# Softmax denominators: a VectorE reciprocal in place of two ScalarE activations

## The chip, the cores and the metric

One Trainium2 chip, all 8 of its cores, one launch. The metric is the device time of the slowest core in microseconds. Each core works on 1024 of the 8192 tokens: four cores share one batch element, and the program of all eight is the same.

## The reference

A "macaron" layer: `x += 0.5*ffn(ln(x))`, `x += attn(ln(x))`, `x += 0.5*ffn(ln(x))` on x of shape 2 x 4096 x 2048, f32. Only the attention matters here:

```
latent_k = h @ Wk.T ; latent_v = h @ Wv.T          # 64 latent dimensions
q_latent = einsum('bthd,hdl->bthl', Q, q_to_latent)  # 16 heads
logits   = q_latent . latent_k / sqrt(64), causal,
           plus 0.5 * (sum of q_latent) * (sum of latent_k) / sqrt(64) in a band of 64 keys
attn     = softmax(logits)
ctx      = attn @ (latent_v @ v_up) ; out = ctx @ Wo.T
```

The softmax's division is the place of the change: the kernel sums the exponentials of each query and multiplies the context row by one over the sum.

## The kernel before

The activations are held transposed, features on partitions and the core's 1024 tokens along the free dimension. A first phase does, for each of the four token blocks of its batch element, layernorm, ffn, layernorm and the latent k and v. Then come the query projection, the attention, the output projection and the second ffn.

The attention runs over 16 heads, and in each head over 32 key tiles `i` of 128 keys plus two iterations to drain. The order of work on each engine is the order in which the helpers are called, since every engine takes its instructions in order and engines meet only at semaphores (`ct` counts TensorE's steps, `cs` ScalarE's, `cv` VectorE's). In iteration `i`:

- VectorE: `emit_outer` (L1363, `ob`) and `emit_select` (L1377, `mr`) make the band term. They need nothing of this iteration.
- TensorE, `emit_iter`: the context product of tile i-2 into `CV` (L1450, keys on the contraction, 65 output rows: 64 of the context and, as row 64, the sum of the exponentials), then the scores of tile i into `PC` (L1471).
- ScalarE copies the 256 leading columns of the scores to SBUF (L1391), VectorE adds the band term (L1399, `madd`), ScalarE takes the exponential of these (L1426) and, without the detour, of the rest (L1419).

A query tile's work ends early, by causality: the columns 0 to 511 of `CV` are complete after tile 19, the columns 512 to 1023 after tile 31. So each head has two epilogues, one for each half of the columns:

- `emit_epi_sums`: VectorE copies 64 rows of `CV` to `cv_sb` (L1277) and the sums to `sums_sb` (L1279, 1x512). Then ScalarE makes the reciprocal as exp(-ln(s)), with two activations on one partition, L1286 (`Ln`) and L1289 (`Exp`), into `rcp_row`.
- `emit_epi_rep`: TensorE multiplies a column of ones with `rcp_row`, so that all 128 partitions hold it (L1304, f32, 1x512, two passes that the trace shows as x2), and VectorE copies that to `rep_sb` (L1311).
- `emit_epi_out`: TensorE multiplies `cv_sb` with `v_up` (L1326), and VectorE multiplies the product with `rep_sb` into `bbuf` (L1337).

For half 0 the three are called at i = 22, 24 and 25 of the same head, ahead of that iteration's own work. For half 1 all three are called together at i = 1 of the next head, ahead of iteration 1 (in the last head, behind everything). There TensorE's order is: the scores of tile 0 of the new head, L1304 and L1326 of the epilogue, then the scores of tile 1. The first step on the head after that, L1083 (called at i = 2), waits for L1337 too. Stages of the next head's queries and bounds (`emit_A_stage`) are spread over i = 2 to 15.

A single table set with `Ln` and `Exp` is loaded once at the start (`preload_set6`, L632).

Of the kernel before, what the change touches and what calls it, by code (L numbers as in the profile page):

```python
# [12 lines left out]
AF = mybir.ActivationFunctionType  # L13
# [624 lines left out]
def build_fused():  # L638
# [38 lines left out]
    with contextlib.ExitStack() as stx:  # L677
# [10 lines left out]
        block = e(nc.Block())  # L688
        preload_set6(block)
        ct, cs, cv = S['ct'], S['cs'], S['cv']  # L690
# [7 lines left out]
        with contextlib.ExitStack() as ph1:  # L698
# [50 lines left out]
            for j in range(4):  # L749
                xq_toks = []  # L750
                for qd in range(4):
# [5 lines left out]
                    def _(sy, j=j, qd=qd, rel=rel, dxn=dx.n):  # L757
                        sy.wait_ge(dx.h, dxn)
                        if rel is not None:
# [7 lines left out]
                _, ln1_ap, mr1 = emit_ln(nc, block, bufs, S, x_chunks, xhat,  # L767
                                         wait0=w0, mrr=mrr1)
# [6 lines left out]
                _, ln2_q, mr2 = emit_ln(nc, block, bufs, S, x_chunks, xhat,  # L775
                                        wait0=w2l, mrr=mrr2)
# [64 lines left out]
        with contextlib.ExitStack() as attn_stack:  # L841
# [21 lines left out]
            sums_sb = ea(nc.sbuf_tensor("sums_sb", [1, NTOK], F32))  # L863
            rep_sb = ea(nc.sbuf_tensor("rep_sb", [128, NTOK], F32))
            rcp_row = ea(nc.sbuf_tensor("rcp_row", [1, NTOK], F32))
# [151 lines left out]
            with contextlib.ExitStack() as ps2:  # L1017
# [252 lines left out]
                def emit_epi_sums(h, half, sc_tok):  # L1270
                    lo, hi = 512 * half, 512 * half + 512
                    @block.vector
                    def _(v, sc_tok=sc_tok, lo=lo, hi=hi,
                          cl=PF['ctx_last']):
                        v.wait_ge(ct.h, sc_tok)
                        v.wait_ge(ct.h, cl)
                        v.tensor_copy(cv_sb[:, lo:hi],  # L1277
                                      CV[0:64, lo:hi]).then_inc(cv.h, 1)
                        v.tensor_copy(sums_sb[:, lo:hi],  # L1279
                                      CV[64:65, lo:hi]).then_inc(cv.h, 1)  # L1280
                    cv.inc(1)
                    s_tok = cv.inc()
                    @block.scalar
                    def _(s, s_tok=s_tok, lo=lo, hi=hi):
                        s.wait_ge(cv.h, s_tok)
                        s.activation(rcp_row[:, lo:hi], sums_sb[:, lo:hi],  # L1286
                                     AF.Ln).then_inc(cs.h, 1)
                        s.wait_ge(cs.h, cs.n + 1)
                        s.activation(rcp_row[:, lo:hi], rcp_row[:, lo:hi],  # L1289
                                     AF.Exp, scale=-1.0).then_inc(cs.h, 1)  # L1290
                    cs.inc(1)
                    return (s_tok, cs.inc())

                def emit_epi_rep(h, half, rcp_tok):
                    lo, hi = 512 * half, 512 * half + 512
                    nxt = A.get(h + 1)
                    ve_war = nxt['b8'] if nxt else 0
                    @block.tensor
                    def _(t, rcp_tok=rcp_tok, ve_war=ve_war, lo=lo, hi=hi,
                          pdf=PF['pdfree']):  # L1300
                        t.wait_ge(cs.h, rcp_tok)
                        t.wait_ge(cv.h, ve_war)
                        t.wait_ge(cv.h, pdf)
                        t.matmul(PA[:, lo:hi], bufs['onesr_f'][:, :],  # L1304
                                 rcp_row[:, lo:hi], start=True,
                                 stop=True).then_inc(ct.h, 1)
                    rep_tok = ct.inc()
                    @block.vector
                    def _(v, rep_tok=rep_tok, lo=lo, hi=hi):
                        v.wait_ge(ct.h, rep_tok)  # L1310
                        v.tensor_copy(rep_sb[:, lo:hi],  # L1311
                                      PA[:, lo:hi]).then_inc(cv.h, 1)
                    return (rep_tok, cv.inc())
# [32 lines left out]
                for h in range(H):  # L1346
# [132 lines left out]
                    for i in range(NT + 2):  # L1479
                        if i == 1 and epi.get('pend') is not None:  # L1480
                            ph, psc = epi.pop('pend')
                            s1 = emit_epi_sums(ph, 1, psc)
                            r1 = emit_epi_rep(ph, 1, s1[1])
                            co1 = emit_epi_out(ph, 1, r1, s1[0],
                                               PF['pdfree'])
                            PF['pdfree'] = co1
                            PF['pb'] = (cv.h, s1[0])
                            PF['pa'] = (cv.h, co1)
                        if h + 1 < H and 2 <= i <= 15:
                            emit_A_stage(h + 1, i - 2)  # L1490
                        if i == 22:
                            epi['sums0'] = emit_epi_sums(h, 0, sc_toks[19])
                        elif i == 24:
                            epi['rep0'] = emit_epi_rep(h, 0,
                                                       epi['sums0'][1])
                        elif i == 25:
                            out0 = emit_epi_out(h, 0, epi['rep0'],
                                                epi['sums0'][0],
                                                PF['pdfree'])
                            PF['pdfree'] = out0  # L1500
# [13 lines left out]
                    if h + 1 < H:  # L1514
                        epi['pend'] = (h, sc_toks[NT - 1])
                    else:
                        s1 = emit_epi_sums(h, 1, sc_toks[NT - 1])
                        r1 = emit_epi_rep(h, 1, s1[1])
                        ctxout_tok = emit_epi_out(h, 1, r1, s1[0],
                                                  PF['pdfree'])  # L1520
# [29 lines left out]
        with contextlib.ExitStack() as f2:  # L1550
# [13 lines left out]
            def wo_cb(m, pap, mm_tok):  # L1564
# [14 lines left out]
            _, ln3_ap, mr3 = emit_ln(  # L1579
                nc, block, bufs, S, x_chunks, xhat3,  # L1580
                wait0=[(cv.h, wo_toks[c]) for c in range(NCH)], mrr=mrr3)
# [98 lines left out]
```

## Time and profile before

| | |
|---|---|
| runs | 3282.74, 3283.88 (median), 3368.11 us |
| profiled execution | 3286.02 us, span of its slowest core 3283.4 us |
| spans of the 8 cores | 3267.2 to 3283.4 us, granted clock 0.747 to 0.749 |
| VectorE busy over the span | 1254.8 us (38%), 2561 instructions |
| ScalarE busy over the span | 869.3 us (26%), 1789 instructions |
| TensorE busy over the span | 2431.0 us (74%), 8607 matmuls |

The share of busy time is an average over stages. The page also prints the span in 40 slices of 82.1 us with one digit each, the busy tenths of an engine in that slice; the attention fills the slices from about the 21st to the 35th. A timeline row gives the start, the duration, the engine, the line, the operation with output and input, and in brackets how long the engine had been idle before it, with what released it.

### The profile page before, as it was taken

To read this page: it belongs to the slowest core of one execution; us is meant where nothing else is said; L and a number is where in the kernel's file an instruction comes from. 1 tells how busy PE (TensorE), PEld (TensorE's weight loads), DVE (VectorE), ACT (ScalarE), POOL (GpSimd) and SP (SyncE) were. 2 spreads that over 40 slices of the span, in tenths; PEclk is the share of its full clock that TensorE was granted. 3 is DMA by queue.
4 is the path that set the end of the run, shared out by engine and by line. 5 is a ranking of instruction groups with operands and counts; after the bars stand their busy time and mean duration, and the time that the engine had idled before them with its cause. 6 is when DMAs were issued, how large, how long until landed. Compare 5 with 4: busy or idle time off the path is not lost.

```text
span 3283.4 us, 29191 instructions; the slowest of 8 cores (3267.2 to 3283.4 us)
## 1 busy us (share of the span) xinstructions
PE 2431.0 (74%) x8607; PEld 863.0 (26%) x8607; DVE 1254.8 (38%) x2561; ACT 869.3 (26%) x1789; POOL 52.2 (2%) x78
## 2 busy tenths in 40 slices
PE   5998669866988679849736666666666666597997
PEld 1333124321432133313212111112221111142333
DVE  2103320243003320331157676666776676412103
ACT  2110211022102201010015455545555554402110
POOL 0000000000000000000000000000000000000000
PEclk8999889887999789979855555555555555598999
DMA  4440334114330344014100000000000000221332
GB/s 128 66 71 1 106 52 77 26 32 120 57 52 0 106 77 77 0 26 69 27 17 1 1 1 1 1 1 1 1 1 1 1 1 1 48 55 19 68 68 102
DMA packets 15263, 127.97 MB, mean 39 GB/s; under 512 B 6433, under 2 KB 6746, under 8 KB 7626
## 3 DMA queue, kind: packets, MB, share of 16 engines
q0 software_dynamic: 6864, 82.28, 14.8%
q1 hardware_dynamic: 8250, 43.83, 3.7%
q8 instruction: 77, 1.26, 0.2%
q14 instruction: 72, 0.59, 0.1%
HBM read 196.53 MB, written 9.27 MB: 63 GB/s over the span
## 4 chain that ended last, share of the span: by engine, by line
PE 58%; DVE 22%; issue 7%; ACT 7%; DMA 4%; DVEq 1%; ACTq 0%; POOL 0%; SPq 0%; POOLq 0%
PE bp_p L319 24%; DVE xhat L243 5%; PE fe_p L574 5%; PE fe_p L516 4%; PE ln_sum L184 4%; PE ln_sum L187 4%; DVE madd L1399 3%; ACT madd L1391 3%; DVE mr L1377 2%; PE CV L1450 2%; PE PA L1304 2%; PE PC L1471 2%; PE bp_p L332 2%; PE bp_cs L289 1%; DVE madd L1200 1%
## 5 line engine op out<-in xcount | busy, mean ns | idle before, releaser
L319 PE MATMUL bp_p<-xhat,wslotP 128*128 128x512 bf16 x2560 | 574.6, 383 | 56.3 <-DVE xhat L243 56.3
L1450 PE MATMUL CV<-probs,vtT 128*65 128x512 bf16 (+3 forms) x768 | 343.7, 512 | 253.2 <-ACT probs L1426 252.6
L1471 PE MATMUL PC<-qlat_h,kaug 65*128 65x512 bf16 (+3 forms) x768 | 348.3, 522 | 8.4 <-DMA qlat_h<-crow_bf 8.4
L319 PEld LDWEIGHTS bp_p<-xhat,wslotP 128*128 128x128 bf16 x2560 | 245.9, 99 | 383.1 <-issue 104.6
L177 ACT ACTIVATE ln_sq<-x_res 128x1024 bf16<-128x1024 f32 x144 | 152.2, 1057 | 723.4 <-DVE x_res L584 317.5
L1426 ACT ACTIVATE probs<-madd 128x256 bf16<-128x256 f32 (+1 forms) x512 | 206.5, 403 | 352.6 <-DVE madd L1399 343.6
L1399 DVE TENSOR_TENSOR madd<-madd,mr 128x256 f32<-128x256 f32 (+1 forms) x512 | 209.3, 409 | 174.5 <-ACT madd L1391 120.6
L359 ACT ACTIVATE bbuf<-bp_p,b_sb 128x1024 bf16<-128x1024 f32 x80 | 89.2, 1114 | 673.5 <-PE bp_p L332 673.5
L1450 PEld LDWEIGHTS CV<-probs,vtT 128*65 128x65 bf16 x768 | 96.4, 134 | 528.8 <-issue 526.0
L1391 ACT ACTIVATE madd<-PC 128x256 f32<-128x256 f32 (+1 forms) x512 | 183.7, 359 | 180.5 <-PE PC L1471 178.9
L1377 DVE COPY_PREDICATED mr<-bandm_sb,ob 128x256 bf16<-128x256 uint8 (+1 forms) x512 | 210.4, 411 | 54.6 <-DVE ob L1363 2.3
L1419 ACT ACTIVATE probs<-PC 128x640 bf16<-128x640 f32 (+5 forms) x384 | 205.8, 536 | 0.0
L413 DVE TENSOR_SCALAR ffn_zsb<-kv_ps,b_sb 8x1024 f32<-8x1024 f32 x4 | 5.1, 1272 | 440.0 <-PE kv_ps L403 440.0
L243 DVE TENSOR_TENSOR xhat<-x_res,ln_rrep 128x1024 bf16<-128x1024 f32 x144 | 163.7, 1211 | 24.1 <-PE ln_rrep L233 24.1
L184 PE MATMUL ln_sum<-x_res,ones_f 128*1 128x512 f32 x288 | 147.9, 595 | 17.7 <-DMA x_res<-xall 9.8
L187 PE MATMUL ln_sum<-x_res,ones_f 128*1 128x512 f32 x288 | 147.9, 595 | 0.0
L1363 DVE TENSOR_SCALAR ob<-qshrepb,ksumT 128x256 bf16<-128x256 bf16 (+1 forms) x512 | 140.8, 275 | 0.0
L1304 PE MATMUL PA<-rcp_row,onesr_f 1*128 1x512 f32 x64 | 65.3, 1121 | 93.1 <-ACT rcp_row L1289 66.9
L200 DVE TENSOR_SCALAR ln_m<-ln_sum 1x1024 f32<-1x1024 f32 x9 | 10.9, 1211 | 320.0 <-PE ln_sq L193 320.0
L319 PE MATMUL bp_p<-bbuf,wslotF 128*128 128x512 bf16 x512 | 113.2, 385 | 18.2 <-DMA wslotF<-woq 18.2
L574 PE MATMUL fe_p<-ffn_vx,wslotP 128*128 128x512 bf16 x512 | 120.1, 400 | 6.6 <-DVE ffn_vx L556 6.6
L1471 PEld LDWEIGHTS PC<-qlat_h,kaug 65*128 65x128 bf16 x768 | 96.0, 128 | 100.4 <-issue 91.9
(170 smaller groups left out, 2010.6 us busy)
## 6 DMA issues: line engine op xcount, KB each, us to landing
x_res<-xall SPq DMA_DIRECT2D x16, 2048.0 KB, 9.0
wslotP<-w1q POOLq DMA_DIRECT2D x16, 2048.0 KB, 16.6
wslotP<-varr POOLq DMA_DIRECT2D x4, 2048.0 KB, 16.1
wslotP<-uarr POOLq DMA_DIRECT2D x4, 2048.0 KB, 16.0
wslotP<-wqq POOLq DMA_DIRECT2D x4, 2048.0 KB, 16.6
wslotF<-woq POOLq DMA_DIRECT2D x4, 2048.0 KB, 14.6
wslotF<-w1q POOLq DMA_DIRECT2D x4, 2048.0 KB, 13.9
yout<-x_res SPq DMA_DIRECT2D x4, 2048.0 KB
```

The source lines that it names most:

```text
L184: t.matmul(p_sum[:, 0:512], bufs['ones_f'][:, 0:1], src_chunks[c][:, 0:512], start=(c == 0), stop=(c == NCH - 1))
L187: t.matmul(p_sum[:, 512:1024], bufs['ones_f'][:, 0:1], src_chunks[c][:, 512:1024], start=(c == 0), stop=(c == NCH - 1))
L243: v.tensor_mul(dst[:, NTOK * c:NTOK * (c + 1)], src_chunks[c], p_rrep[:, :]).then_inc(cv.h, 1)
L319: mi = t.matmul(P[par][:, 512 * half:512 * half + 512], lhsT, rhs_sb[:, NTOK * k + 512 * half: NTOK * k + 512 * half + 512], start=(k == 0 ...
L574: mi = t.matmul(P[par][:, 512 * half:512 * half + 512], lhsT, vx[:, NTOK * j + 512 * half: NTOK * j + 512 * half + 512], start=(j == 0), s ...
L1377: v.copy_predicated(mr_sb[r][:, 0:lead], bandm_sb[:, 256 * r:256 * r + lead], ob_sb[i % 2][:, 0:lead]).then_inc(cv.h, 1)
L1391: s.activation(madd2_sb[i % 2][:, 0:lead], PC[:, qlo + dlt:qlo + dlt + lead], AF.Copy).then_inc(cs.h, 1)
L1399: v.tensor_tensor(madd2_sb[i % 2][:, 0:lead], madd2_sb[i % 2][:, 0:lead], mr_sb[i % 4][:, 0:lead], ALU.add).then_inc(cv.h, 1)
L1419: s.activation(probs[i % 2][:, a:b], PC[:, a + dlt:b + dlt], AF.Exp).then_inc(cs.h, 1)
L1426: s.activation(probs[i % 2][:, qlo:qlo + lead], madd2_sb[i % 2][:, 0:lead], AF.Exp).then_inc(cs.h, 1)
L1450: mi = t.matmul(CV[0:65, a:b], vtT[:, 66 * j:66 * j + 65], probs[j % 2][:, a:b], start=(j == 0), stop=last)
L1471: mi = t.matmul(PC[:, a + dlt:b + dlt], kaug[0:65, 128 * i:128 * i + 128], ql[0:65, a:b], start=True, stop=True)
```

## The change

In `emit_epi_sums` the two ScalarE activations are taken out. In their place VectorE does one `reciprocal` on the same 1x512 row, from `sums_sb` into `rcp_row`, directly behind its copy of the sums and with a wait for that copy. The function returns a token of VectorE's semaphore, and `emit_epi_rep` makes TensorE wait for that one.

```diff
                         v.tensor_copy(sums_sb[:, lo:hi],
                                       CV[64:65, lo:hi]).then_inc(cv.h, 1)
+                        v.wait_ge(cv.h, cv.n + 2)
+                        v.reciprocal(rcp_row[:, lo:hi],
+                                     sums_sb[:, lo:hi]).then_inc(cv.h, 1)
                     cv.inc(1)
                     s_tok = cv.inc()
-                    @block.scalar
-                    def _(s, s_tok=s_tok, lo=lo, hi=hi):
-                        s.wait_ge(cv.h, s_tok)
-                        s.activation(rcp_row[:, lo:hi], sums_sb[:, lo:hi],
-                                     AF.Ln).then_inc(cs.h, 1)
-                        s.wait_ge(cs.h, cs.n + 1)
-                        s.activation(rcp_row[:, lo:hi], rcp_row[:, lo:hi],
-                                     AF.Exp, scale=-1.0).then_inc(cs.h, 1)
-                    cs.inc(1)
-                    return (s_tok, cs.inc())
+                    return (s_tok, cv.inc())
...
-                        t.wait_ge(cs.h, rcp_tok)
+                        t.wait_ge(cv.h, rcp_tok)
                         t.wait_ge(cv.h, ve_war)
                         t.wait_ge(cv.h, pdf)
```

## Rows read from the trace of the kernel before

**Rows 1.** The page's part 2: busy tenths and granted clock, 40 slices

```profile
DVE  2103320243003320331157676666776676412103
ACT  2110211022102201010015455545555554402110
PEclk8999889887999789979855555555555555598999
```

**Rows 2.** Busy time by stretch: attention's main part; length, busy by engine, clock

```profile
1740.00:2850.00 1110.00, 719.88 (x1807) 222.10 (x1807) 762.80 (x1943) 571.48 (x1453) 15.08 (x16) 0.50 0.00 1
```

**Rows 3.** Groups by line and shape, 1480 to 2850 us: busy, mean ns | idle before

```profile
L1304 PE MATMUL PA<-rcp_row,onesr_f 1*128 1x512 f32 x64 | 65.3, 1121 | 93.1 <-ACT rcp_row L1289 66.9 <-ACT madd L1391 26.2
L1289 ACT ACTIVATE rcp_row<-rcp_row 1x512 f32<-1x512 f32 x32 | 20.1, 629 | 2.9
L1286 ACT ACTIVATE rcp_row<-sums_sb 1x512 f32<-1x512 f32 x32 | 20.1, 629 | 30.2 <-DVE sums_sb L1279 30.2
```

**Rows 4.** Timeline at a head's start: epilogue of half 1

```profile
2132.89 0.68 DVE L1279 COPY sums_sb<-CV 1x512 f32<-1x512 f32 x1
2133.66 0.63 ACT L1286 ACTIVATE rcp_row<-sums_sb 1x512 f32<-1x512 f32 x1 [0.89 <-DVE sums_sb L1279]
2134.38 0.63 ACT L1289 ACTIVATE rcp_row<-rcp_row 1x512 f32<-1x512 f32 x1
...
2135.37 2.04 PE L1304 MATMUL PA<-rcp_row,onesr_f 1*128 1x512 f32 x2 [4.19 <-ACT rcp_row L1289]
...
2137.52 0.69 DVE L1311 COPY rep_sb<-PA 128x512 f32<-128x512 f32 x1 [3.95 <-PE PA L1304]
...
2139.01 0.38 ACT L1391 ACTIVATE madd<-PC 128x256 f32<-128x256 f32 x1 [4.00 <-PE PC L1471]
```

**Rows 5.** Timeline of the same head's iterations 22 and 23: half 0

```profile
2113.69 0.69 DVE L1279 COPY sums_sb<-CV 1x512 f32<-1x512 f32 x1
...
2114.30 0.27 DVE L1363 TENSOR_SCALAR ob<-qshrepb,ksumT 128x256 bf16<-128x256 bf16 x1
2114.47 0.63 ACT L1286 ACTIVATE rcp_row<-sums_sb 1x512 f32<-1x512 f32 x1 [0.89 <-DVE sums_sb L1279]
2114.67 0.43 DVE L1377 COPY_PREDICATED mr<-bandm_sb,ob 128x256 bf16<-128x256 uint8 x1
2115.19 0.63 ACT L1289 ACTIVATE rcp_row<-rcp_row 1x512 f32<-1x512 f32 x1
2115.73 0.36 ACT L1391 ACTIVATE madd<-PC 128x256 f32<-128x256 f32 x1
...
2116.18 2.04 PE L1304 MATMUL PA<-rcp_row,onesr_f 1*128 1x512 f32 x2 [1.63 <-ACT madd L1391]
2116.25 0.43 DVE L1399 TENSOR_TENSOR madd<-madd,mr 128x256 f32<-128x256 f32 x1 [1.15 <-ACT probs L1419]
...
2117.63 0.42 DVE L1399 TENSOR_TENSOR madd<-madd,mr 128x256 f32<-128x256 f32 x1 [0.23 <-ACT probs L1419]
...
2118.32 0.69 DVE L1311 COPY rep_sb<-PA 128x512 f32<-128x512 f32 x1 [0.27 <-PE PA L1304]
```

**Rows 6.** Groups by line and shape, VectorE, whole span: same columns as rows 3

```profile
L1399 DVE TENSOR_TENSOR madd<-madd,mr 128x256 f32<-128x256 f32 x448 | 190.6, 426 | 160.6 <-ACT madd L1391 106.8 <-ACT probs L1419 30.7 <-DVE mr L1377 1.1
...
L1399 DVE TENSOR_TENSOR madd<-madd,mr 128x128 f32<-128x128 f32 x64 | 18.7, 292 | 13.9 <-ACT madd L1391 13.8
...
L1054 DVE COPY vtT<-ones_bf 128x1 bf16<-128x1 bf16 x32 | 4.7, 147 | 0.0
...
L456 DVE RECIPROCAL ffn_rc<-ffn_ss 128x8 f32<-128x8 f32 x5 | 1.0, 203 | 0.5
...
L458 DVE TENSOR_SCALAR ffn_rc<-ffn_rc 128x8 f32<-128x8 f32 x5 | 0.9, 171 | 0.5
...
L945 DVE COPY km<-kmt 1x1 f32<-1x1 f32 x1 | 0.1, 141 | 0.1
```

## Prediction

> **What bounds the kernel now.** I read four views, from coarse to fine. The page's busy tenths come first, to see in which stage the edited lines lie and what that stage looks like [rows 1]. From about the 21st slice to the 35th VectorE is busy at 6 to 7 tenths, ScalarE at 4 to 5, and TensorE is granted a clock of 0.5, its lower level of 1.2 GHz. The sums by stretch say the same in us: of 1110 us, 763 are VectorE's, 571 ScalarE's and 720 TensorE's [rows 2]. No engine is full. So what sets the pace is a ring of waits: scores, copy, add of the band term, exponential, and so on. In such a stage the busy time that an engine gains or loses is worth little by itself; what counts is how long the steps on the ring take, one behind the other.
>
> Then the groups by line, to see whether anybody waits for the edited lines [rows 3]. The two activations take 629 ns each, 32 times. TensorE stands idle for 93.1 us in front of L1304, the matmul that reads `rcp_row`. 66.9 us of that are put down to L1289, 16 times 4.2 us: that is the epilogue of half 1, at the head's start. The other 26.2 us (16 times 1.64) are put down to L1391, the copy of scores. But in the timeline L1304 starts at 2116.18, which is 0.36 us after the end of L1289 (2115.82), just as in the other half (2135.01 to 2135.37) [rows 4, 5]. So here too it was L1289 that released it. In both halves the row of reciprocals is waited for.
>
> Last the two timelines, to see who stands behind. At the head's start [rows 4] everything stands: before L1304 TensorE was idle for 4.19 us, before L1311 VectorE for 3.95 us, and before the next copy of scores ScalarE for 4.00 us, because the scores of tile 1 are behind L1304 on TensorE's queue. At i = 22 [rows 5] the next band add of VectorE (2116.25) had waited 1.15 us, for a copy of scores that stood behind the two activations on ScalarE.
>
> **What is removed.** 64 activations of 0.63 us, 40 us of ScalarE. As busy time it is worth nothing (ScalarE is half idle), but as a link of the chain all of it counts. From the end of the copy of the sums to the end of L1289 are 2135.01 - 2133.57 = 1.44 us in half 1 and 2115.82 - 2114.38 = 1.44 us in half 0.
>
> **What is added.** 32 reciprocals on VectorE of 1x512 f32, duration R. The wait for the own copy costs about 0.1 us: the reciprocal that the ffn does behind such a wait has 0.5 us of idle time before its five instances [rows 6]. The wait of TensorE changes its semaphore only; the two waits behind it stay, so I leave the 0.36 us from the last result to L1304 as they are.
>
> **The duration R.** This is what decides. The trace has one reciprocal, 128x8 f32, 203 ns [rows 6]; a 1x512 one is not in it. An ordinary operation costs one element per 1.05 ns: (426 - 292)/128 [rows 6]. What the reciprocal needs per element comes from setting its 203 ns against short operations. Against L458, a multiplication by a constant of the same 128x8 f32 (171 ns), it is 32 ns longer for 8 elements, 4.0 ns each, together with the ordinary 1.05 about 5.05 ns. Then R = 203 + 504 x 5.05 = 2.75 us. Against a copy of a single element (L1054, 147 ns), the seven further elements cost 56 ns, 8.0 ns each, and R = 203 + 504 x 8.0 = 4.24 us. The ends: L945 (141 ns, f32 but one partition) gives 62/7 = 8.9 ns and R = 4.67 us; and if the whole difference were a fixed one, with 1.05 ns per element, R = 203 + 504 x 1.05 = 0.73 us. The two middle readings both fit one point, and I can't separate them. I take the mean of 5.05 and 8.0, 6.5 ns: R = 203 + 504 x 6.5 = 3.48 us.
>
> On this the Trainium skill has a rule (VectorE: DVE Perf Modes, section "First, the fixed hardware budget"): the reciprocal is an iterative division with a repeat count of 8, so not an ordinary one-slice operation. Read as eight cycles of its 0.96 GHz for each element, that is an estimate of 8.3 ns per element and 4.4 us for 512; the sum below would then be 99 us. The one row of the reciprocal agrees if its fixed part is a copy's, and doesn't if it is a multiplication's. I keep it as a rival.
>
> **Half 1, on the chain.** VectorE was idle in that time, so it loses no work, but the chain is longer: R + 0.1 in place of 1.44. L1304, L1326, the scores of tile 1, L1311 and L1337 all shift by R - 1.34 us. Nothing absorbs it, since all three engines stand. Per case 3.48 - 1.34 = 2.14 us, and there are 16: 15 between heads, and the last one ahead of the output projection, whose weight loads wait for the attention's end.
>
> **Half 0, at i = 22.** Queued behind the reciprocal on VectorE are `ob`, `mr` and the add of tile 22; ScalarE's exponential and then TensorE's context product wait for that add. In numbers [rows 5]: the reciprocal starts at 2114.47 and ends at 2114.47 + R. `ob` can start 0.08 us before that end (as it did before the end of L1279), and the add follows 0.90 us behind the start of `ob` (0.37 to `mr`, as in the row, and 0.53 for `mr`: its 0.43 us and 0.1 us for the wait). That is 2115.29 + R in place of 2116.25: R - 0.96. The next add came 1.38 us after (2117.63 - 2116.25) and will again. L1304 starts at 2114.83 + R and its result is there at 2116.97 + R; VectorE is through with the second add at 2117.01 + R. So L1311, which before waited 0.27 us for TensorE, starts at about 2117.02 + R in place of 2118.32: R - 1.30. TensorE's own shift is 2114.83 + R - 2116.18 = R - 1.35. All that comes after i = 24 hangs on these, and so half 0 costs R - 1.30 = 2.18 us, 16 times. That ScalarE has no activations ahead of its copy any longer is contained in it; it is why the shift is not R - 0.1.
>
> **The sum.** 16 x (R - 1.34) + 16 x (R - 1.30) = 32 R - 42.2. With R = 3.48: 111.4 - 42.2 = 69 us. The profiled execution took 3286.0 us with a span of 3283.4; the median of the runs shown is 3283.9, so the difference is added to the median without a correction: 3353 us, 2.1% more. VectorE's busy time should grow by 32 x 3.48 = 111 us, ScalarE's fall by 40 us. TensorE stays at clock 0.5 in this stage (it was there before, with fewer pauses), and at the clock of before in the others, whose work isn't touched.
>
> **Rivals.**
> - *Eight cycles per element.* R between 4.24 and 4.67 from rows (8.0 to 8.9 ns, about eight times the 1.05 of an ordinary element). 32 R - 42.2 = 93 to 107 us: 3377 to 3391 us. For it: the ratio comes out at a whole 8 against a copy. Against it: the multiplication of the same shape leaves only 5. Chance 0.27.
> - *Full rate, the rival on the other side.* The 32 to 60 ns by which the reciprocal exceeds other short operations are a longer pipeline, paid once, and R = 0.73 us. Then 32 x 0.73 - 42.2 = -19 us: 3265 us, not slower, 0.6% less, within 2%. One short row can't exclude it. The change is free at R = 1.32 us (2.2 ns per element) and 2% slower from R = (65.7 + 42.2)/32 = 3.37 us. Against it: even the nearest row asks for a fixed cost of 195 ns, and the other short operations of [rows 6] take 171 ns at most in all. Chance 0.12.
> - *Half 0 is absorbed.* If the reciprocal at i = 22 lay beside ScalarE's work without holding up the ring, only half 1 would be left: 16 x 2.14 = 34 us, 3318 us. For it: VectorE had 1.15 us of idle time there. Against it: the reciprocal is longer than that by far, and the add is directly behind it in order. Chance 0.05.
> - The likeliest, R between 2.75 and 4.2 and both halves on the chain: 46 to 92 us, 3330 to 3376 us. Chance 0.56.
>
> **How the numbers follow.** The predicted time is that of the likeliest, 3353 us. The range for 8 in 10 leaves out the full rate and the absorbed half, reaches a little below 3330 for the reading of the multiplication, and above takes in most of the eight-cycle rival: 3322 to 3388. A measurement of this kernel tells about 2% from no change. Slower by over 2% needs R above 3.37 us: the whole of the eight-cycle case (0.27) and somewhat under half of the likeliest, whose middle lies just above that point and whose lower part stands on the same kind and size of operation (0.25), 0.52. Faster by over 2% is in none of the cases; I leave 0.02 for an effect that I don't see. Within 2%: 0.46.
>
> **What the profile after would show.** One group of 32 RECIPROCALs, 1x512, on VectorE: its mean is R, and 32 R - 42.2 should be the growth of the span. In the timeline at the head's start L1304 should start 0.36 us after the reciprocal's end, and the idle time before it should grow from 4.19 us by R - 1.34. At i = 22 the add of the band term should follow 0.8 us after the reciprocal's end, with no wait for ScalarE, and L1311 should have no wait for TensorE. The prediction is wrong in its mechanism if the growth differs from that formula with the measured R by over 10 us; it is wrong only in a size if the formula holds and R is another.

## The result, and the profile after

The kernel got slower by 2.2% over ten runs of each (ratio 1.0221, 95% interval 1.0153 to 1.0289). On another chip, in the experiments below, it was 1.8% (1.0178, 1.0147 to 1.0208). In some executions the cores of one die had a lower granted clock and took longer (for which the last row of the table below uses cores 4 to 7 alone); the ratios leave such executions out but still hold one milder case in each series, 3394.8 us of the changed kernel in the first and 3303.6 us of the kernel before in the second, and without these two both series give 1.9%, 63 and 62 us. The four lowest times of the first series are 3344.7 to 3348.2 us, against 3281.2 to 3286.3 for the five lowest before. So the change costs about 62 us. The profiled execution took 3345.96 us (3286.02 before, 59.9 more); its span on the slowest core was 3344.3 us (3283.4, 60.9 more).

The page of the changed kernel, head and parts 1 and 2, lines of VectorE, ScalarE and the clock. To compare: [rows 1] and the table of the kernel before.

```profile
span 3344.3 us, 29013 instructions; the slowest of 8 cores (3330.4 to 3344.3 us)
...
PE 2414.9 (72%) x8493; PEld 862.2 (26%) x8607; DVE 1360.5 (41%) x2593; ACT 828.7 (25%) x1725; POOL 52.5 (2%) x78
...
DVE  2003220332013400331267777777777777512103
ACT  2110211022102210200034444444444444302110
...
PEclk8999889888988799969655555555555555599999
```

VectorE has 32 instructions and 105.7 us more, ScalarE 64 instructions and 40.6 us less. (TensorE shows 8493 matmuls where it had 8607. The weight loads are 8607 in both, so some records of matmuls are missing, not work.) In the attention's slices VectorE's digits went from mostly 6 and 7 to 7, ScalarE's from 4 and 5 to 4. Elsewhere single digits differ too, because a slice is now 83.6 us long and the borders lie elsewhere. The clock in the attention stayed at 0.5, so a lower clock isn't what costs the time there.

Two groups by line of the changed kernel, busy and mean ns, then the idle time before them and its releasers; to compare with [rows 3]. The second is from the view of 1740 to 2910 us:

```profile
L1282 DVE RECIPROCAL rcp_row<-sums_sb 1x512 f32<-1x512 f32 x32 | 106.9, 3341 | 3.3
...
L1298 PE MATMUL PA<-rcp_row,onesr_f 1*128 1x512 f32 x64 | 65.3, 1121 | 156.6 <-DVE rcp_row L1282 98.2 <-DVE ob L1357 58.4
```

This pair has nearly the whole result. The reciprocal takes 3.341 us. TensorE's idle time ahead of the matmul that reads the row (L1304 before, L1298 now) grew from 93.1 to 156.6 us, by 63.5 us, about what the kernel lost. It grew in both halves: in half 1 from 66.9 to 98.2 us, 16 times 1.96; in half 0 from 26.2 to 58.4 us, 16 times 2.01. (`ob` is named as the releaser in half 0 since it starts just before the reciprocal ends; the timeline below shows what it waited for.)

The timeline of the changed kernel at a head's start, as [rows 4]:

```profile
2154.94 0.69 DVE L1279 COPY sums_sb<-CV 1x512 f32<-1x512 f32 x1
2155.73 3.34 DVE L1282 RECIPROCAL rcp_row<-sums_sb 1x512 f32<-1x512 f32 x1
...
2159.42 2.04 PE L1298 MATMUL PA<-rcp_row,onesr_f 1*128 1x512 f32 x2 [6.19 <-DVE rcp_row L1282]
...
2161.57 0.69 DVE L1305 COPY rep_sb<-PA 128x512 f32<-128x512 f32 x1 [2.50 <-PE PA L1298]
...
2163.07 0.38 ACT L1385 ACTIVATE madd<-PC 128x256 f32<-128x256 f32 x1 [8.24 <-PE PC L1465]
```

From the start of the copy of the sums to TensorE's matmul are 4.48 us in place of 2.48, and to the next copy of scores 8.13 in place of 6.12. ScalarE stood idle there for 8.24 us in one piece. That is its 4.00 us of before, the 0.89 us before the Ln and the 1.35 us of the two activations with their gap [rows 4], and 2.0 us by which the chain got longer.

And at i = 22 of the same head, as [rows 5]:

```profile
2133.95 0.69 DVE L1279 COPY sums_sb<-CV 1x512 f32<-1x512 f32 x1
...
2134.74 3.34 DVE L1282 RECIPROCAL rcp_row<-sums_sb 1x512 f32<-1x512 f32 x1
2138.01 0.17 DVE L1357 TENSOR_SCALAR ob<-qshrepb,ksumT 128x256 bf16<-128x256 bf16 x1
...
2138.43 2.04 PE L1298 MATMUL PA<-rcp_row,onesr_f 1*128 1x512 f32 x2 [3.64 <-DVE ob L1357]
2138.82 0.43 DVE L1393 TENSOR_TENSOR madd<-madd,mr 128x256 f32<-128x256 f32 x1
...
2139.34 0.42 ACT L1420 ACTIVATE probs<-madd 128x256 bf16<-128x256 f32 x1 [5.06 <-DVE madd L1393]
...
2140.20 0.42 DVE L1393 TENSOR_TENSOR madd<-madd,mr 128x256 f32<-128x256 f32 x1 [0.23 <-ACT probs L1413]
...
2140.65 0.69 DVE L1305 COPY rep_sb<-PA 128x512 f32<-128x512 f32 x1
```

The add of the band term (2138.82) has no wait for ScalarE any longer; now ScalarE's exponential waits 5.06 us for it. L1305 has no wait for TensorE: VectorE is now last at both places, at the second one narrowly (its second add ends at 2140.62, L1298 at 2140.47). From the copy of the sums to L1305 are 6.70 us in place of 4.63, 2.07 more.

### The profile page after: what moved, and what is told of

Read it like the earlier page. It is cut to its first block, busy times and chain, and to the rows that moved or that the text cites. A ratio compares the mean times of both kernels' runs of the same rounds, so it can differ in the third digit from the quotient of the medians.

```text
span 3344.3 us, 29013 instructions; the slowest of 8 cores (3330.4 to 3344.3 us)
## 1 busy us (share of the span) xinstructions
PE 2414.9 (72%) x8493; PEld 862.2 (26%) x8607; DVE 1360.5 (41%) x2593; ACT 828.7 (25%) x1725; POOL 52.5 (2%) x78
## 4 chain that ended last, share of the span: by engine, by line
PE 56%; DVE 25%; issue 8%; ACT 6%; DMA 4%; DVEq 1%; ACTq 0%; POOL 0%; SPq 0%; POOLq 0%
PE bp_p L319 23%; DVE xhat L243 5%; PE fe_p L574 4%; PE fe_p L516 4%; PE ln_sum L184 4%; DVE madd L1393 4%; PE ln_sum L187 4%; DVE rcp_row L1282 3%; ACT madd L1385 3%; DVE mr L1371 2%; PE CV L1444 2%; PE PC L1465 2%; PE bp_p L332 2%; PE bp_cs L289 1%; DVE madd L1200 1%
## 5 line engine op out<-in xcount | busy, mean ns | idle before, releaser
L319 PE MATMUL bp_p<-xhat,wslotP 128*128 128x512 bf16 x2503 | 565.1, 383 | 63.7 <-DVE xhat L243 57.6
L1298 PE MATMUL PA<-rcp_row,onesr_f 1*128 1x512 f32 x64 | 65.3, 1121 | 156.6 <-DVE rcp_row L1282 98.2
L584 DVE TENSOR_TENSOR x_res<-x_res,fe_p 128x1024 f32<-128x1024 f32 x80 | 97.7, 1221 | 59.6 <-PE fe_p L574 59.6
```

The source lines that it names most:

```text
L319: mi = t.matmul(P[par][:, 512 * half:512 * half + 512], lhsT, rhs_sb[:, NTOK * k + 512 * half: NTOK * k + 512 * half + 512], start=(k == 0 ...
```

## The experiments

Ratios and lowest times stand against the kernel before, which ran on the same chip with each group. "In the attention" is the time from the first to the last of the 32 copies L1277, from the profile. The kernel before has one profile with which all the others are compared. Since the cores of one execution differ by up to 5 us in that time, and the slowest core isn't always the same one, the difference in the last column is taken core by core and averaged over the eight. The rows of that copy carry it (number, minimum, median and maximum in ns, first and last start in us): the kernel before, then the changed one.

```profile
L1277 DVE CAST cv_sb<-CV x32: 675/676/683, 1751.1 to 2841.6; 64x512 bf16<-64x512 f32 x32
```

```profile
L1277 DVE CAST cv_sb<-CV x32: 675/676/683, 1750.2 to 2900.0; 64x512 bf16<-64x512 f32 x32
```

1090.5 us before, 1149.8 us after, 59.3 more on the slowest core of each, and 60.5 to 63.6, mean 61.5, on the same cores. So nearly all of the loss is between these two copies. Ahead of the first of them the kernels are 0.9 us apart. The last epilogue, of half 1, has its reciprocal behind the second: 31 of the 32 cases count here.

| kernel | ratio (95%) | lowest (kernel before), us | in the attention, slowest core, us | difference, same cores, us |
|---|---|---|---|---|
| the change again | 1.0178 (1.0147 to 1.0208) | 3343.6 (3280.7) | 1151.2 | +61.2 |
| half 1 alone | 1.0107 (1.0093 to 1.0122) | 3310.7 (3279.4) | 1119.4 | +29.1 |
| half 0 alone | 1.0107 (1.0092 to 1.0122) | 3316.1 (3279.4) | 1124.6 | +34.2 |
| copy in place of the reciprocal | 0.9918 (0.9903 to 0.9932) | 3253.0 (3279.4) | 1061.7 | -28.0 |
| reciprocal twice | 1.0531 (1.0518 to 1.0545) | 3454.5 (3279.4) | 1257.9 | +168.3 |
| spread, then reciprocal | 1.0105 (1.0059 to 1.0152) | 3320.7 (3280.7) | 1128.9 | +38.1 |
| Ln from PSUM, Exp after the spreading | 0.9816 (0.9801 to 0.9832) | 3220.5 (3280.7) | 1032.7 | -57.0 |
| half 1's epilogue spread out | 0.9962 (0.9948 to 0.9976) | 3268.0 (3280.7) | 1076.5 | -12.2 |
| the same in the changed kernel | 1.0139 (1.0103 to 1.0175) | 3331.8 (3280.7) | 1137.7 | +46.2 |
| Exp after the spreading, and half 1's epilogue spread out | 0.9781 (0.9763 to 0.9798) | 3207.9 (3280.7) | 1019.5 to 1021.9 (cores 4 to 7) | -68.4 (cores 4 to 7) |

Three ratios are about 0.1% low by the execution of 3303.6 us of the kernel before, which they hold (the change again; spread, then reciprocal; the same in the changed kernel). For these the text goes by the other times.

**Each half alone.** The condition `half == 1` (or 0) chooses VectorE's reciprocal; the other half keeps its two activations, and TensorE waits for the semaphore that belongs to it.

```diff
+                    if half == 1:
+                        @block.vector
+                        def _(v, s_tok=s_tok, lo=lo, hi=hi):
+                            v.wait_ge(cv.h, s_tok)
+                            v.reciprocal(rcp_row[:, lo:hi],
+                                         sums_sb[:, lo:hi]).then_inc(cv.h, 1)
+                        return (s_tok, (cv.h, cv.inc()))
...
```

> Only the epilogue of half 1 (at the head's start) has the reciprocal on VectorE; half 0 keeps the two activations. Chain theory: 16 x (R - 1.34) = 16 x 2.00 = 32 us over before. Rival (half 0 is absorbed, half 1 carries the whole growth): 61 us. Rival (half 1 is absorbed because VectorE was idle there): 0 us.

> Only the epilogue of half 0 (i = 22) has the reciprocal on VectorE. Chain theory: 16 x (R - 1.30) = 16 x 2.04 = 33 us over before, and with half 1 alone it adds up to the whole change. Rival (absorbed beside ScalarE's work): 0 us.

Both cost 35 us by the median time of the whole kernel. In the attention it is 29.1 us for half 1, of which 15 cases lie in that stretch (1.94 each), and 34.2 us for half 0, 16 cases (2.14 each). Neither half is absorbed, and neither carries the whole. Half 0 cost slightly more and half 1 slightly less than R - 1.30 and R - 1.34.

**The change again**, to see whether the halves add up.

> The changed kernel once more, beside the kernel before on one chip, to see whether its growth is the sum of the two halves (35 + 35 = 70 us). Chain theory, with R = 3.341 us: 64.7 us. If the halves merely add: 70 us. If they share some waiting time: about 60 us.

About 62 us, and 61.2 us in the attention. There the halves sum to 63.3 us and the formula gives 16 x 2.04 + 15 x 2.00 = 62.6: they add within some 2 us. By the medians of whole runs they would be 70. Of the kernel with half 1 alone, one execution took 3310.65 us and the three others 3317.2 to 3317.7. Only the first was profiled, so where the 6 us of the others lie isn't known. The whole kernels therefore don't settle whether the halves add exactly; the profiles of the attention do, and the points below rest on these.

**A copy in place of the reciprocal**, in the changed kernel. The reciprocal is left out of the computation.

```diff
-                        v.reciprocal(rcp_row[:, lo:hi],
-                                     sums_sb[:, lo:hi]).then_inc(cv.h, 1)
+                        v.tensor_copy(rcp_row[:, lo:hi],
+                                      sums_sb[:, lo:hi]).then_inc(cv.h, 1)
```

> In the changed kernel the reciprocal is replaced by a VectorE copy of the same row; the reciprocal is left out of the computation. Chain theory: the formula 32 R - 42.2 with R = about 0.42 us (f32 in SBUF at the rate of the 1x1024 scaling by a constant, 0.68 us, halved in length) gives -29 us against before. Rival (what slows the changed kernel is not the duration but the move itself, the changed semaphore or the additional VectorE instruction): at least as slow as before.

The copy takes 415 ns, and the kernel is 28 us faster than before. With R = 0.415 the formula gives 32 x 0.415 - 42.2 = -29 us. So the move itself, the added instruction and the other semaphore cost no more than the formula already holds for them, and the loss is one of duration. It also says what a reciprocal as short as a copy would have been worth.

**The reciprocal twice.**

```diff
                                      sums_sb[:, lo:hi]).then_inc(cv.h, 1)
+                        v.wait_ge(cv.h, cv.n + 3)
+                        v.reciprocal(rcp_row[:, lo:hi],
+                                     sums_sb[:, lo:hi]).then_inc(cv.h, 1)
...
```

> The changed kernel with the reciprocal done twice, one behind the other. Chain theory: all of the second is on the chain too, 32 x (3.34 + 0.1) = 110 us on top of the changed kernel, 171 to 175 us over before. Rival (half of it would be hidden by waits that grow elsewhere): about 55 us on top.

174 us over before. In the attention it is 106.8 us over the changed kernel, in 31 cases 3.45 each; one more reciprocal and its wait are 3.44. With this and the copy the formula holds within 4 us at R = 0.4, 3.3 and 6.8 us: over this range it is a straight line, and each us of VectorE at that place is a us of the kernel, once per epilogue.

**How long a reciprocal is.** 16 of them ahead of the first head of the kernel before, from and to `rep_sb`, each shape twice.

> The kernel before, with 16 reciprocals more ahead of the first head, each shape twice: 1x1, 1x8, 1x64, 1x256, 1x512, 128x1, 128x64, 128x512. A straight line through 203 ns (8 elements) and 3341 ns (512) has 6.23 ns per element and 153 ns fixed: 159, 203, 552, 1747, 3341 ns, and the same on 128 partitions. Rival (not a line: a cheap start, then eight cycles per element): 1x64 near 0.6 us but 1x256 above 2 us.

Groups by line and shape, VectorE, mean ns of one:

```profile
L1351 DVE RECIPROCAL rep_sb<-rep_sb 128x512 f32<-128x512 f32 x2 | 6.7, 3353 | 0.2
L1351 DVE RECIPROCAL rep_sb<-rep_sb 1x512 f32<-1x512 f32 x2 | 6.7, 3341 | 0.2
L1351 DVE RECIPROCAL rep_sb<-rep_sb 1x256 f32<-1x256 f32 x2 | 3.5, 1742 | 0.2
L1351 DVE RECIPROCAL rep_sb<-rep_sb 128x64 f32<-128x64 f32 x2 | 1.1, 553 | 0.2
L1351 DVE RECIPROCAL rep_sb<-rep_sb 1x64 f32<-1x64 f32 x2 | 1.1, 540 | 0.2
...
L1351 DVE RECIPROCAL rep_sb<-rep_sb 1x8 f32<-1x8 f32 x2 | 0.4, 192 | 0.2
L1351 DVE RECIPROCAL rep_sb<-rep_sb 128x1 f32<-128x1 f32 x2 | 0.3, 164 | 0.2
L1351 DVE RECIPROCAL rep_sb<-rep_sb 1x1 f32<-1x1 f32 x2 | 0.3, 151 | 0.2
```

It is a straight line: (3341 - 1742)/256 = 6.25 ns per element and (1742 - 540)/192 = 6.26, with some 142 ns fixed on one partition (3341 - 512 x 6.25) and 153 on 128. An ordinary element is 1.05 ns [rows 6], so it is six of these, not eight and not five. 128 partitions cost 12 to 13 ns more than one.

On this the Trainium skill (VectorE: DVE Perf Modes, section "First, the fixed hardware budget") speaks of an iterative division with a repeat count of 8. That the operation isn't at full rate is what the rows show too. A reading as eight cycles per element, 8.3 ns, is excluded by the 6.25.

**Spread first, then the reciprocal.** In the changed kernel TensorE spreads the sums as they are, and VectorE's reciprocal of the 128x512 result stands where the copy to `rep_sb` was.

```diff
-                        v.wait_ge(cv.h, cv.n + 2)
-                        v.reciprocal(rcp_row[:, lo:hi],
-                                     sums_sb[:, lo:hi]).then_inc(cv.h, 1)
...
-                                 rcp_row[:, lo:hi], start=True,
+                                 sums_sb[:, lo:hi], start=True,
...
-                        v.tensor_copy(rep_sb[:, lo:hi],
-                                      PA[:, lo:hi]).then_inc(cv.h, 1)
+                        v.reciprocal(rep_sb[:, lo:hi],
+                                     PA[:, lo:hi]).then_inc(cv.h, 1)
```

> The changed kernel with the reciprocal moved behind L1304: TensorE spreads the raw sums over 128 partitions, and VectorE's reciprocal of the 128x512 result, from PSUM, takes the place of the copy to rep_sb. The reciprocal is as long on 128 partitions as on one (3353 and 3341 ns). Chain theory: the row's part of the chain loses 1.44 us against before, the copy's part gains 3.35 - 0.69 = 2.66 us: 1.2 us per epilogue, 39 us over before, and so 26 us less than the changed kernel. Rival (the reciprocal's place doesn't matter, only that VectorE does it): as the changed kernel, 65 us over before. Rival (the scores of tile 1 are no longer behind it and cover it): 0 to 20 us.

```profile
L1302 DVE RECIPROCAL rep_sb<-PA 128x512 f32<-128x512 f32 x32 | 107.5, 3358 | 40.6 <-PE PA L1295 40.1
```

38 us over before by the three lowest times (3320.7 to 3322.1 us), and 38.1 us in the attention (31 x 1.2 = 37 expected). The same busy time on VectorE as in the changed kernel, 107.5 against 106.9 us, costs 23 us less in another place, because there it takes the place of a copy. What counts is the difference on the chain, not the time on the engine.

**Ln from PSUM, Exp after the spreading.** The kernel before, with ScalarE doing more of the epilogue and not less. (A wait of the next head's first context product for `rcp_row`'s Ln, and one of the Ln for the last L1304, are part of it.)

```diff
-                        v.tensor_copy(sums_sb[:, lo:hi],
-                                      CV[64:65, lo:hi]).then_inc(cv.h, 1)
...
-                        s.activation(rcp_row[:, lo:hi], sums_sb[:, lo:hi],
+                        s.activation(rcp_row[:, lo:hi], CV[64:65, lo:hi],
                                      AF.Ln).then_inc(cs.h, 1)
-                        s.wait_ge(cs.h, cs.n + 1)
-                        s.activation(rcp_row[:, lo:hi], rcp_row[:, lo:hi],
-                                     AF.Exp, scale=-1.0).then_inc(cs.h, 1)
...
-                        v.tensor_copy(rep_sb[:, lo:hi],
-                                      PA[:, lo:hi]).then_inc(cv.h, 1)
+                        s.activation(rep_sb[:, lo:hi], PA[:, lo:hi],
+                                     AF.Exp, scale=-1.0).then_inc(cs.h, 1)
```

> The kernel before, but ScalarE's Ln reads the sums from PSUM (no copy L1279), TensorE spreads the logarithm over the partitions, and ScalarE's Exp(-x) of the 128x512 result takes the place of VectorE's copy to rep_sb and of the 1x512 Exp. Chain theory: at the head's start L1304 can start 1.6 us earlier, at i = 22 too; with the copy L1311 replaced about 1.7 us per epilogue, 32 times: -54 us against before. Rival (the 128x512 Exp on ScalarE, about 0.6 us, stands in the ring itself): some -35 us.

1.8% faster than before, 60 us, and 57.0 us in the attention, 1.84 per epilogue with 1.7 expected. The groups by line of this kernel, 1480 to 2850 us:

```profile
L1299 PE MATMUL PA<-rcp_row,onesr_f 1*128 1x512 f32 x64 | 65.3, 1121 | 39.7 <-ACT rcp_row L1285 38.4 <-DVE cv_sb L1277 1.1
...
L1285 ACT ACTIVATE rcp_row<-CV 1x512 f32<-1x512 f32 x32 | 18.9, 590 | 1.3 <-PE CV L1449 0.6
L1309 ACT ACTIVATE rep_sb<-PA 128x512 f32<-128x512 f32 x32 | 18.8, 589 | 40.9 <-PE PA L1299 40.8
```

TensorE's idle time ahead of the spreading matmul fell from 93.1 [rows 3] to 39.7 us. The Exp of the 128x512 result takes 0.59 us, where VectorE's copy of it took 0.69 [rows 4], so the second activation of the row, and the copy of the sums, are simply gone.

**Half 1's epilogue spread out**, in the kernel before and in the changed one.

```diff
                         if i == 1 and epi.get('pend') is not None:
-                            ph, psc = epi.pop('pend')
-                            s1 = emit_epi_sums(ph, 1, psc)
-                            r1 = emit_epi_rep(ph, 1, s1[1])
+                            ph, psc = epi['pend']
+                            s1 = epi['s1'] = emit_epi_sums(ph, 1, psc)
+                            PF['pb'] = (cv.h, s1[0])
+                        if i == 2 and epi.get('pend') is not None:
+                            r1 = epi['r1'] = emit_epi_rep(ph, 1, s1[1])
+                        if i == 3 and epi.get('pend') is not None:
                             co1 = emit_epi_out(ph, 1, r1, s1[0],
                                                PF['pdfree'])
...
-                        if h + 1 < H and 2 <= i <= 15:
-                            emit_A_stage(h + 1, i - 2)
+                            epi.pop('pend')
+                        if h + 1 < H and 4 <= i <= 17:
+                            emit_A_stage(h + 1, i - 4)
```

> The kernel before, with the epilogue of half 1 spread as that of half 0 is: sums at i = 1, L1304 at i = 2, output at i = 3, and the stages of the next head's queries two iterations later. Chain theory: TensorE no longer holds the scores of tile 1 behind L1304, and of the 4.00 us that ScalarE stood idle there about 3.5 us come back, 16 times: -56 us. Rival (the stall only moves to i = 2, where L1304 holds the context product of tile 0 for the same time): 0 to -15 us.

Only 12 us (0.4%): my theory expected 56, and the number is the rival's. The rival's reason is only a part of it. The starts of the copies of scores L1391 in one head, from that of tile 0 on, by the timelines (us, worked out from their rows):

```
tile              1      2      4      7      15     16     17     18     29
before          7.73  10.91  18.21  25.45  41.58  46.57  48.09  49.49  67.86
spread out      3.64   8.07  13.18  23.10  39.43  41.54  43.22  48.53  66.90
difference     -4.09  -2.84  -5.03  -2.35  -2.15  -5.03  -4.87  -0.96  -0.96
```

The same head's copy of tile 2, before and spread out:

```profile
2142.19 0.39 ACT L1391 ACTIVATE madd<-PC 128x256 f32<-128x256 f32 x1 [1.35 <-PE PC L1471]
```

```profile
2132.20 0.38 ACT L1391 ACTIVATE madd<-PC 128x256 f32<-128x256 f32 x1 [2.97 <-PE PC L1471]
```

The stall at tile 1 did go, 4.1 us of it. A part came back at once, as the rival says: at tile 2 ScalarE now waits 2.97 us for the scores in place of 1.35, and the gain fell to 2.8 us. At tile 4 the head was 5.0 us ahead, since the stages of the next head's queries start two tiles later. From tile 4 to tile 7, which now hold them, the gain fell to 2.4 us. The rest went at the pause between two copies of some 5 us, in which VectorE waits for the DMA that brings back the bounds (1.89 us before, 2.10 spread out) and then works on them for 1.9 us (L1255 and L1258, 1.21 and 0.68 us). Before it was between tiles 15 and 16, now it is between tiles 17 and 18. The two tiles that it passed over take 1.4 to 1.5 us each without stages (before) and 1.7 to 2.1 with them. 0.96 us were left in this head, and 12.2 us in the whole attention. The edit moved the epilogue and the stages together, and no run moves one without the other. So how much each of them gave back is read from one head's rows and isn't shown by an experiment.

> The changed kernel with the epilogue of half 1 spread over i = 1 to 3 as in the staggered kernel. Chain theory: VectorE takes its instructions in order, so the reciprocal holds up the band terms and adds behind it wherever the epilogue stands, 32 x 2.04 = 65 us over the staggered kernel, 53 us over before. Rival (spread out, TensorE's and ScalarE's work covers the reciprocal at the head's start): about 33 us over the staggered kernel, 21 us over before.

50 us over before (3331.8 to 3334.0 us, with 3280.7 to 3285.6 before), and in the attention 58.4 us over the spread-out kernel without the change (56.2 to 60.6 on the eight cores), where 62.6 were expected. In this arrangement the reciprocal costs 58.4/31 = 1.9 us per epilogue, a little less than the formula's 2.0, and not the half that the rival says. In the trace of this kernel a reciprocal at a head's start runs from 2148.77 to 2152.11 us, `ob` starts at 2152.04 and the add at 2152.85, and ScalarE's exponential waits 4.53 us for that add: the band term of the tile stands behind the reciprocal here too.

**Both together**, the spread-out epilogue and the Exp after the spreading.

> Both edits together. If they shorten different waits, the gains add: about -110 us against before. Rival (both remove the same idle time at the head's start): no more than half 0's share of the first, -27 us, on top of the second alone: -83 us.

2.2% faster than before, 0.9781 (0.9763 to 0.9798), with the three lowest times at 3207.9 to 3211.6 us: 72 us. 60 + 13 = 73, so the gains add, and the rival (27 us on top of the second edit's 13) fell. The 110 us expected failed all the same, because they held 56 us for the second edit. It is the fastest version here.

## Why the prediction was right

**The duration R**: 3.341 us where I took 3.48, 4% less. It came as a mean of two readings of one short row, 5.05 and 8.0 ns per element; the measured 6.25 is between them, and that it was so near their mean is luck. Neither reading was right by itself: the one charged too much of the 203 ns to the fixed part, the other too little. A reciprocal of one element on 128 partitions takes 164 ns, 17 more than the copy of one element (147) that I used for the upper reading. That reading's "whole 8" was generous too: 8.0/1.05 is 7.6. The two rivals that hung on it, eight cycles per element and full rate, both fell by the row of the changed kernel.

**The sum**: with the measured R the formula 32 R - 42.2 gives 64.7 us. The span grew by 60.9, the lowest runs of the two series by 63 and 62. The formula is 2 to 4 us too high, the prediction of 69 us some 6 to 8. Of that, 32 x 0.14 = 4.5 us are R.

**Half 1**: R - 1.34 = 2.00 us predicted, 2.00 in the timeline shown (4.48 - 2.48), 1.94 in the kernel with this half alone, 1.96 in TensorE's idle time. The 0.36 us from the last result to L1304 stayed as they were (2159.07 to 2159.42).

**Half 0**: R - 1.30 = 2.04 us predicted, 2.07 in the timeline and 2.14 in the kernel with this half alone. The add follows 0.74 us after the reciprocal's end with no wait for ScalarE, and L1305 waits for nothing. Two small terms cancel here: the add comes 0.08 us sooner than I had it, and I had let L1311 start 0.08 us before the second add's end (2117.01, where the durations give 2117.09), which L1305 doesn't do (2140.62 to 2140.65). The rival in which half 0 is absorbed fell by the kernel with half 0 alone: 35 us.

**What was not on the chain**: ScalarE's 40 us of relief count only as the link that they were, the 1.44 us per epilogue in the formula, and not once more as relief. The kernel with the copy gained 28 us, but this is the shorter chain (1.44 us against 0.5 per epilogue); and the kernel in which ScalarE kept two activations and took over one 128x512 pass gained 60.

**The chances**: 0.52 for slower by over 2% and 0.46 for within 2% were for two cases with the border at R = 3.37 us. The measured R is just below it, and 62 to 63 us are just below the 65.7 us that 2% are. The two series gave 2.2% and 1.8%, each with an interval that holds 2%, so the ratios don't say which side it was on; the lowest runs say 1.9%.

## What to carry to other kernels

Before you move an operation from one engine to another, ask whether it is a link of a chain that somebody waits for. If it is, the engine's busy share doesn't matter, and only the durations count: here 1.44 us (two activations with their waits) against 3.44 (one reciprocal with its wait). An operation that the trace shows only in a tiny shape should be measured in the shape that is wanted, since a short row separates the fixed part from the rate badly. And a stall that is taken away comes back elsewhere if other waits stand behind it: of the 4.1 us at tile 1, 0.96 were left at the head's end. Follow the gain through the iterations before you count it 16 times.

## What the runs showed of the hardware

- VectorE's reciprocal in f32 takes 6.25 ns per element of a partition and 142 to 153 ns fixed, in SBUF, and nearly as much from PSUM (3358 ns for 128x512, 3353 from SBUF). ScalarE's Ln and Exp of 1x512 take 629 ns each from SBUF [rows 3]. From PSUM the Ln of 1x512 takes 590 ns and the Exp of 128x512 589.
- A reciprocal of 128x512 is nearly as long as one of 1x512, 3353 and 3341 ns: 128 times the elements for 12 ns.
